# Another order of four chunks, and the last batch's projection in single fp16 passes: LayerNorm, rotary attention and an int8 gated FFN on one core

## The reference

```
xn = layernorm(x)                                  # x: 4 batches, 1024 tokens, 256 wide
q = rope(xn @ Wq) / 4 ; kv = rope(xn @ Wkv)        # 16 heads of 16; keys and values are the same tensor
attn = softmax(q @ kv^T) @ kv                      # per head, 1024 x 1024
out = x + attn @ Wout + bout + (silu(xn @ Wg^T) * (xn @ Wu^T)) @ Wd^T     # Wg, Wu, Wd int8-valued / 127, hidden 768
```

## Time and profile before

| | |
|---|---|
| median of 3 runs | 833.54 us |
| profiled execution, its time | 833.63 us |
| its span, first to last instruction | 831.8 us |
| mean granted TensorE clock | 0.994 |
| busy: PE, DVE, ACT, POOL | 799.3, 736.4, 691.0, 267.3 us |

### The profile page before, as it was taken

One profiled execution on the slowest core, in us unless ns is written; L12 is line 12 of the kernel. 1 busy time (PEld: TensorE's weight loads), 2 busy tenths in 40 slices (PEclk: granted clock), 3 DMA queues, 4 the chain that ended last, 5 costly groups with the idle time before them and its releaser, 6 DMA issues.

```text
span 831.8 us, 19133 instructions
## 1 busy us (share of the span) xinstructions
PE 799.3 (96%) x7316; PEld 296.1 (36%) x7316; DVE 736.4 (89%) x891; ACT 691.0 (83%) x1268; POOL 267.3 (32%) x504
## 2 busy tenths in 40 slices
PE   4888999999999999999999999999999999999997
PEld 2344555445333233333333333333333333333234
DVE  6776888888899999999999999999999999999702
ACT  5565455545799999999999999999999999999982
POOL 3877678886120001101222222222222222222210
PEclk9998999999999999999999999999999999999999
DMA  9455655565111111111221122221222112221222
GB/s 311 120 129 113 140 117 112 113 119 129 42 33 35 29 37 30 31 30 45 57 58 50 49 54 58 53 51 49 55 56 58 51 49 52 58 55 50 83 72 75
DMA packets 111680, 60.55 MB, mean 73 GB/s; under 512 B 71372, under 2 KB 101900, under 8 KB 111588
## 3 DMA queue, kind: packets, MB, share of 16 engines
q1 hardware_dynamic: 111588, 59.32, 28.6%
HBM read 28.57 MB, written 16.90 MB: 55 GB/s over the span
## 4 chain that ended last, share of the span: by engine, by line
PE 90%; ACT 3%; issue 2%; DVE 2%; POOL 2%; DMA 1%; SPq 0%; DVEq 0%; ACTq 0%; POOLq 0%
PE ps L753 34%; PE ps L770 19%; PE ps L735 15%; PE ps L629 9%; PE ps L643 4%; ACT arena L1014 2%; PE ps L608 1%; PE ps L607 1%; PE ps L606 1%; DMA arena<-w_up_dram 1%; PE ps L678 1%; PE ps L781 1%; PE ps L797 1%; PE ps L783 1%; PE ps L782 1%
## 5 line engine op out<-in xcount | busy, mean ns | idle before, releaser
L1169 DVE TENSOR_REDUCE negmax<-ps 128x2 f32<-128x1024 f32 x512 | 589.0, 1216 | 9.8 <-PE ps L770 6.4
L1014 ACT ACTIVATE arena<-ps 128x512 f32<-128x512 f32 x1024 | 555.5, 595 | 32.4 <-PE ps L735 10.6
L753 PE MATMUL ps<-arena 128*32 128x256 f32 x4072 | 326.5, 392 | 2.4 <-issue 2.2
L735 PE MATMUL ps<-qs,ks 51*128 51x512 f16 x1024 | 197.9, 382 | 3.3 <-ACT arena L1014 2.1
L770 PE MATMUL ps<-ks,qs 48*128 48x512 f16 x972 | 189.4, 386 | 0.0
L753 PEld LDWEIGHTS ps<-arena 128*32 128x32 f32 x4072 | 80.4, 107 | 128.0 <-issue 126.9
L770 PEld LDWEIGHTS ps<-ks,qs 48*128 48x128 f16 x972 | 46.5, 92 | 195.1 <-DVE negmax L1169 142.3
L629 PE MATMUL ps<-arena,side 128*128 128x512 f16 x384 | 92.4, 391 | 3.8 <-DVE side L1114 3.8
L1434 POOL TENSOR_TENSOR arena<-arena,x_all 128x256 f32<-128x256 f32 x22 | 16.1, 731 | 230.3 <-ACT arena L1035 230.3
L735 PEld LDWEIGHTS ps<-qs,ks 51*128 51x128 f16 x1024 | 50.7, 93 | 77.8 <-ACT arena L1014 45.7
L1365 POOL TENSOR_TENSOR mparts<-rowmax,munit 128x16 f16<-128x16 f32 x32 | 7.1, 221 | 210.3 <-DVE rowmax L1179 210.3
(11 more groups left out here) (115 smaller groups left out, 511.6 us busy)
## 6 DMA issues: line engine op xcount, KB each, us to landing
parts_d<-arena SPq DMA_DIRECT2D x64, 128.0 KB
x_all<-x_dram SPq DMA_DIRECT2D x8, 512.0 KB, 9.1
qs<-parts_d SPq DMA_DIRECT2D x64, 64.0 KB, 1.9
ks<-parts_d SPq DMA_DIRECT2D x64, 64.0 KB, 1.9
o_d<-arena SPq DMA_DIRECT2D x124, 32.0 KB
arena<-o_d SPq DMA_DIRECT2D x24, 128.0 KB
arena<-inv_d SPq DMA_DIRECT2D x48, 64.0 KB
out_dram<-arena SPq DMA_DIRECT2D x24, 128.0 KB, 1.8
```

The lines of the kernel that those rows point to most:

```text
L735: mm = pe.matmul(ps[:, score_bank(place(p, kt, 2 * half + a)), :], ks[ring][top:top + ROWS, kt * P:(kt + 1) * P], qs[ring][top:top + ROWS, ...
L753: mm = pe.matmul(ps[32 * j:32 * j + 32, 7, cols], vstage[pl % 2][:, j % 2, kt, :], probs[PER_STEP * (kt % PBUF) + j][:, cols], start=(kt = ...
L1014: act.activation(probs[PER_STEP * (kt % PBUF) + j], ps[:, score_bank(place(p, kt, j)), :], ACT.Exp).then_inc(exp_done, 1)
L1169: dve.tensor_reduce(negmax[pl % 2][:, h, :, kt], ps[:, bank:bank + 2, :], AX.X, ALU.max, negate=True).then_inc(max_done, 1)
```

## The change

It has two halves.

**Chunks.** In SyncE's queue `turn_qk` of chunks 1 to 6 now stands ahead of `turn_x` of the next chunk. `store_chunk` writes the groups in the order 0, 2, 1, 3, and `load_pair` waits for two groups instead of four. `moments` of 8 tiles (not 12) stands in chunk 0, of 16 (not 12) in chunk 1; `add_ffn` of chunk 0 moves behind `gated` 1 of chunk 1; ScalarE calls Silu once right behind the roots, which loads its table there. GpSimd's `low_qk` of chunk 0 stands behind all six `low_hid`. The leads start one `gate_up` later in chunk 2, one earlier in chunk 7.

**End.** The front's 24 passes, now fp16 over split operands, go to pair 30's slots 7 to 10, 14, 15 and pair 31's slots 0 to 2, 10 to 13, one or two in each. Tile 21 is projected in pair 30's slots 11 to 13 and tile 23 in pair 31's slots 5 to 8, tile 22 in slot 3, all in fp16. The front's operands are loaded one pair earlier, divided and split by GpSimd (`divide_front`); VectorE splits the back's.

```diff
-LATE_AT = {6: 22, 11: 23}
-FRONT_AT = {0: 2, 1: 3, 2: 4, 4: 5, 7: 6, 8: 7, 13: 0, 14: 1}
+LATE_TILES = (PAIRS - LAG - 1, PAIRS - LAG + 1)
+LATE_AT = {(PAIRS - 2, 11): (0, range(0, 2)), (PAIRS - 2, 12): (0, range(2, 4)), (PAIRS - 2, 13): (0, range(4, 6)),
+           (PAIRS - 1, 5): (1, range(0, 2)), (PAIRS - 1, 6): (1, range(2, 3)), (PAIRS - 1, 7): (1, range(3, 5)),
+           (PAIRS - 1, 8): (1, range(5, 6))}
...
+            def tile_passes(n, k, bank, passes):
+
+                if passes[0] == 0:
+                    pe.wait_ge(divided, CREDIT + n + 1)
+                    if n == LATE_TILES[1]:
+                        pe.wait_ge(late_done, 1)
...
             for c in range(NCHUNK):
+                if c + 1 == NCHUNK:
+                    turn_rows(0, 0)
+                    load_mrows(0, 0)
+                if c:
+                    turn_qk(c)
                 if c + 1 < NCHUNK:
                     turn_x(c + 1)
-                else:
-                    turn_rows(0, 0)
-                    load_mrows(0, 0)
-                turn_qk(c)
+                if c == 0:
+                    turn_qk(0)
                 store_chunk(c // CPB, c % CPB)
...
-                if p == PAIRS - 2:
-                    sp.wait_ge(inv_stored[0], 16 * QH * (PAIRS - RING) // 2)
-                    load_last(0, front_in)
...
+                if p == PAIRS - 3:
+                    load_last_o(0, front_in)
+                    load_last_inv(0, front_in)
                 if rows:
                     turn_rows(p + 1, j + 1)
...
+            p = PAIRS - 1
             store_o(p - 1, p - 1)
-            sp.wait_ge(divided, CREDIT + p - LAG + 1)
-            load_tile(*tile_of(p - LAG + 2)[0:2], (p - LAG + 2) % 2)
+            sp.wait_ge(divided, CREDIT + LOOP_TILES)
+            load_tile(*tile_of(LOOP_TILES + 1)[0:2], (LOOP_TILES + 1) % 2)
...
+            n = LAST - LAG
+            divide(n, n % 2)
+            divide_front()
+            add_tile(n, n % 2, n)
+            split_max(PAIRS - 1, RING - 1)
```

More of the change, by code:

```diff
@@ L285, in build @@
         o_stored = [sem(f"o_stored{i}") for i in range(2)]
+        sums_in = [sem(f"sums_in{i}") for i in range(2)]
         inv_done = sem("inv_done")
@@ L366, in store_chunk @@
                 sp.wait_ge(qk_turned, 32 * (c + 1))
-                for g in range(4):
+                for g in (0, 2, 1, 3):
                     for k in range(NPART):
@@ L396, in load_pair @@
             def load_pair(p, ring):
-                if p % PPB == 0:
-                    for g in range(4):
+                if p % (PPB // 2) == 0:
+                    for g in (p % PPB * 2 // PPB, HG + p % PPB * 2 // PPB):
                         sp.wait_ge(parts_stored[g], 16 * NPART * CPB * (p // PPB + 1))
@@ L508, in load_last, with load_last_inv @@
                     sp.dma_start(olast[k][0:rows, g, :], o_d[BATCH - 1, g, 0:rows, tok]).then_inc(landed, 16)
+            def load_last_inv(g, landed):
+                rows = P if g == 0 else BACK_ROWS
+                for k in range(CPB):
+                    tok = slice(k * CHUNK, (k + 1) * CHUNK)
                     src = inv_groups[BATCH - 1, g, 0:rows // DH, tok]
@@ L695, in _ @@
                 gate_up(c, 0)
-                gate_up(c, 1)
                 units = lead_units(c)
[L698 to L702, removed]
+                if units:
+                    pe.wait_ge(rope_read, CT * (c + 1))
+                for j in range(1, KH):
+                    if j - lead_at(c) in range(len(units)):
+                        lead(units[j - lead_at(c)])
                     gate_up(c, j)
-                for n in units[UNITS:]:
+                for n in units[KH - lead_at(c):]:
                     lead(n)
@@ L800, in project_back @@
             def project_back(t):
-                pe.matmul(last_out(t), olast[t // CT][0:BACK_ROWS, 1, t % CT * P:(t % CT + 1) * P], wo[0:BACK_ROWS, 1, :],
-                          start=False, stop=False)
+                for i in range(3):
+                    last_pass(t, 1, BACK_ROWS, i)
             def step(turn, ls, last_turn=False):
@@ L881, in _ @@
                 project_back(t)
-            pe.wait_ge(wo_scaled, 2)
+            pe.wait_ge(wo_split, 4)
             pe.wait_ge(normed, 1)
-            for t in range(BT):
+            for t in LAST_ORDER:
                 rows = slice(t // CT * HEAD_ROWS, (t // CT + 1) * HEAD_ROWS)
@@ L1200, in _ @@
                 gated(c, 0)
[L1201 to L1203 removed]
                 units = lead_units(c)
[L1205 to L1207 removed]
+                for j in range(1, KH):
+                    if j - lead_at(c) in range(len(units)):
+                        n = units[j - lead_at(c)]
                         maxima(0, n // 2, n % 2, LEAD_BANK)
                     gated(c, j)
[L1210 to L1211 removed]
+                    if c == 1 and j == 1:
+                        for t in range(CT):
+                            add_ffn(0, t)
+                    elif c == 1:
+                        moments(4 * CT + 3 * (j - 2), 3)
                     if c == 0 and j in (3, 4):
@@ L1388, in _ @@
                     low_hid(c, j)
-                    if c == 0 and 1 <= j <= CT:
-                        low_qk(0, j - 1)
+                if c == 0:
+                    for t in range(CT):
+                        low_qk(0, t)
             def stage_values(p, batch, slot, pair):
@@ L1441, in slot @@
                 for tile in tiles:
-                    if not isinstance(tile[0], int) or tile[0] < LOOP_TILES:
-                        add_tile(*tile, tile[0])
+                    add_tile(*tile, tile[0])
                 q = j + 1
```

210 lines of the change are left out of this document (119 added, 91 removed).

## The result

The changed kernel took 840.63 us, median of 4 (838.44 to 840.92), against 833.43 (833.08 to 833.87) for the kernel before: 1.008, 95% interval 1.0066 to 1.0093, slower by 5.5 to 7.8 us. On a second chip it was 1.0093 (1.0079 to 1.0108). Forecast were 836.2 and a range up to 839.0. The sign was right, the size (2.6 instead of 7.2) too small by nearly a factor of three. The profiled execution has a span of 838.8 and took 840.66.

The account below looks back on a forecast made before the run. TensorE and VectorE were taken as full from 222 to 782 us, ScalarE as the bound in pairs 30 and 31. Terms -0.5 -1.5 -4.5 +6.5 +2.5 +1.0 +0.4 -1.3 = +2.6 on 833.63 gave 836.2 us, range 830.5 to 839.0.

Parts of the forecast that it names:

- ScalarE as the bound: Pair 31: with single fp16 passes replacing fp32 work, ScalarE's exponentials set the time; -4.5 us.
- tile 23's wait: Pair 31, slot 5: TensorE waits 6.6 us because tile 23's load stands behind pair 30's stores; +6.5 us.
- the clock behind it: Pair 31: TensorE restarts at low clock after the wait for tile 23; +2.5 us, between 0 and 2.8.
- The wait for x: Before chunk 2's `project`: x lands at 64.9, TensorE waits 7 to 9 us; with later gains, chunk 3 -0.5 us.
- rival D: Chunks 3 to 6: x turned last is late there too, 0.8 us each, 1.5 in chunk 2; 840.9 us, chance 0.11.
- Chunk 7: Chunk 7: leads one `gate_up` earlier take away most of the 1.7 us wait at the last lead; -1.5 us.
- the front's loads ... +1.0, between 0 and 2: Start of pair 30: loads ahead of the small transpose make the maxima's rows 1.5 us late; +1.0 us, between 0 and 2.
- two passes in each of nine slots of pair 30 fit under ScalarE: Pair 30: a slot with two passes takes TensorE 1.12, just under ScalarE's 1.13, so no cost was counted.
- Tile 21's wait of 0.4: Pair 30, slot 11: tile 21 is projected from about 789.0 but divided at 789.34; +0.4 us.
- The tail: After pair 31: 24 fp16 passes replace the back's 16 fp32 matmuls, with fewer last adds; -1.3 us, between -0.8 and -2.3.
- Rival A: Chunk 2 and pair 31: both waits come but the clock costs nothing; 830.9 us, chance 0.22 in all its degrees.
- B: Pair 31: rival in which tile 23 is in time and the end keeps its gain; 827.2 us, chance 0.09.

Follow-up runs that it names:

- e_swap2: Changed kernel with tile 23's load and the store of tile 21's result ahead of pair 30's stores in SyncE's queue; 830.39 us.
- e_best2: Changed kernel with x first in chunk 1, tile 23's load and tile 21's store ahead of pair 30's stores, front's loads in slot 28; 827.59 us.
- e_xfirst: Changed kernel with chunk 1's transposes of x for chunk 2 put back ahead of those of q and k; 1.3 to 2.4 better than the changed kernel.
- e_onepass: As `e_loads28`, with the second front pass left out in six slots of pair 30 (those products missing from the output); 837.62 us.
- e_swap: Changed kernel with only tile 23's load moved ahead of pair 30's stores in SyncE's queue; no time given in the text.
- e_chunks: Kernel before with only the change's chunk half, the end as before; 832.0 us, ratio 0.9991 to the kernel before.
- e_loads28: Changed kernel with the front's four transfers issued one pair earlier, in SyncE's slot 28 behind `load_mrows(29)`; 837.94 us.
- e_lead7: Changed kernel with one lead of chunk 7 moved from in front of the last `gate_up` to behind it; 841.12 us.
- after_again: The changed kernel unedited, measured again; 841.46 us.
- e_loads: Changed kernel with the front's four transfers put behind `load_mrows(30)` instead of ahead of `turn_rows(30)`; no time given in the text.
- e_end: Changed kernel with chunks 0 to 7 as in the kernel before, so only the end half of the change; 841.35 us.
- e_best3: As `e_best2`, plus chunk 7's lead moved as in `e_lead7`; 829.48 us.
- best2_again: The kernel of `e_best2` measured once more, on another chip; 826.60 us.

## Why the prediction was wrong in its size

*Pair 31: the mechanism right, the sum nearly so.* Forecast were -4.5 for ScalarE as the bound, and +6.5 and +2.5 for tile 23's wait and the clock behind it: +4.5. Measured are -4.3 with the waits removed (`e_swap2`, `e_best2`), a wait of 7.6 in the first profile, and +4.9 there in all. Of 4.3 + 4.9 = 9.2 the wait leaves 1.6 for the clock (1.5 to 3.5 in the other profiles): the longer wait and the cheaper clock offset each other. The wait goes with SyncE's issue of pair 30's four stores and of the load's first transfer behind them. It is 6.2 where these took 2.3, as in the kernel before (`e_xfirst`, `e_onepass`), and 7.0 to 7.8 where they took 3.1 to 3.8. In the first profile the load went out at C + 3.9 instead of the C + 2.5 of the earlier trace rows. Why the issue takes longer in some executions is not shown.

*Chunks: mechanism right, sum by luck.* The wait for x, its release by a transpose, a stretch of low clock, chunk 2 without further waits, and x turned last hidden in chunks 3 to 6 (22.5 each; rival D) all came. But TensorE got to `project(2)` at 62.5, not 57. Of this 2.4 is the first profile's late `project(1)` (36.57 against 34.20); for the rest `gated` had waited for GpSimd. `e_swap` has the starts of the kernel before (`project(1)` at 34.21): there TensorE is ready at 59.7 and x comes at 64.35, for 57 and 64.9 forecast. When x lands was right, when TensorE would want it was not. So the wait was 4.3 (3.5 to 4.8 in the others with this order), not the 7 to 9 that I had named as the sign. In the first profile the low clock also began before that wait, not behind it, and lasted longer than in the earlier trace rows; in `e_chunks` it began only at the wait's end, at 66.2. The transposes took 66.77 - 57.29 = 9.5 from first issue to `project`, between my 10.3 and the 8.3 that the Trainium skill's 261 GB/s (DMA: Bandwidth & Descriptors, "Latency and other measured facts") would give by the same sum, an estimate. Chunk 7 brought 0.2 instead of 1.5. It is an edit for which I named no next wait. Together -1.1 (`e_chunks`) instead of -2.0.

*The failed step: "the front's loads ... +1.0, between 0 and 2".* The wait came, 1.2 to 1.8. What I left out is what I had counted after the two long waits: the clock. It fell here too in four of seven profiles. Against `e_loads28` pair 31 starts 1.3 to 1.5 later where the clock held, inside my range, and 3.2 to 3.3 later where it fell. By the medians the whole term is about 3 (`e_loads28` against `e_lead7` and `after_again`), above my upper bound. I had the clock fall only after waits of 4 us and more and called the one case. The trace of the kernel before had a second, behind a wait of 2.33 (see the last section), and I overlooked it.

*The other failed step: "two passes in each of nine slots of pair 30 fit under ScalarE".* I had 0.9 + 2 x 0.11 = 1.12, just under ScalarE's 1.13. The 0.9 holds (787.98 - 787.09 = 0.89), but two passes up to the next scores take 0.32, not 0.22: the slot is 1.21, and nine of them cost 0.9. I had put this at nothing. The first pass of a slot is free (1.14, `e_onepass`), the second is not.

*Small ones.* Tile 21's wait of 0.4 did not come, since all of pair 30 was late; in `e_onepass`, with pair 30 on time, it was 0.7. The tail gave 0.9 (last values to end of span: 12.6 before, 11.7 after) for a forecast of 1.3.

The sum as the runs have it: -1.1 (chunks) + 3.0 (front's loads, clock included) + 0.9 (double passes) + 5.0 (pair 31) - 0.9 (tail) = +6.9, against 6.7 to 7.8 from the ratios 1.008 and 1.0093. The terms are from different executions and chips, so the closeness is partly luck. Of the 4.3 by which my sum fell short, 2.0 are the front's loads, 0.9 the double passes, 0.9 the chunks and 0.5 pair 31; the tail's 0.4 and tile 21's 0.4 cancel. In the first profile the late start (+1.6) stood in for a clock that held.

Rival A is refuted (the clock was low at both places, and in four profiles at pair 30 too), B too (tile 23 was not in time), but B's number was near the worth of a repair: 827.2 forecast for tile 23 in time, 830.4 measured. That repair took tile 21's store as well, and the rest is mostly the front's loads, the double passes and the smaller gain of the chunks. Rival D's 840.9 stands next to the measured 840.6 by luck: its mechanism, x late in chunks 3 to 6, did not come.

## What to carry to other kernels

A wait taken from the bound engine is worth only the distance to the next chain. Before counting it, write down what is late next, as here in chunk 7 (1.7 removed, 0.2 gained) and after tile 23's load (7.6 removed, 5.5 in its place). In a queue with a fixed order every load that is pulled forward is a delay for what stands behind it: look for the queue's idle stretch (here one pair earlier) rather than the nearest free place. And price a short stall of TensorE with the clock it may lose: where the clock fell behind a wait of 1.5 to 1.8 us, the two came to more than 3.

## What of the hardware was unexpected

The clock fell to 0.5 after short waits, and not always. The kernel before shows it too (TensorE, then a window):

```profile
53.03 8.75 PE L629 MATMUL ps<-arena,side 128*128 128x512 f16 x32 [2.33 <-DVE side L1114]
```

```profile
54.30:57.70 3.40, 3.40 (x9) 1.19 (x8) 1.71 (x6) 1.71 (x4) 3.40 (x4) 0.50 0.03 5
```

In pair 30 it stayed at 1.00 behind 1.2 to 1.3 us and behind 1.54 (`e_loads`), and was 0.50 for 3.4 us behind 1.47 (`e_end`) and 1.7 to 1.8 (`e_lead7`, `e_swap`, `after_again`). Behind the 1.65 of chunk 7 it held in the kernel before, `e_end` and `e_lead7`, and fell in `e_best3`. In `project(3)` it held behind 2.35 (`e_xfirst`) and fell to 0.67 behind 2.13 (`best2_again`). What decides between them the runs don't show.

The executions of one kernel scatter by more than the edits to the chunks are worth: 831.5 to 835.0 for the kernel before on one chip, `project(0)` between 13.0 and 15.0 us in the profiles with identical code ahead of it.
